# Two layer norms moved from VectorE to ScalarE, and the rotation of the keys from GpSimd to VectorE

## What is computed

```
x = x + layernorm(attention(layernorm(x)))
x = x + layernorm(ffn(layernorm(x)))

attention(x):                       # 16 heads of 128
    q = rope(x @ Wq.T)              # per head
    k, v = split(x @ Wkv.T)         # one key and one value for all heads
    kh, vh = running sums over the tokens of (x @ Wkvh.T) * exp(cumsum(log_sigmoid(x @ Wg.T)))
    k of head h = rope(k * kh[h]),  v of head h = v * vh[h]
    softmax(q k / sqrt(128), causal) v, heads joined, @ Wout.T
ffn(x):                             # 1024 hidden, ternary weights in groups of 64
    gate, up = split(x @ Wgu.T);  h = silu(gate) * up;  rms_norm(h) @ Wproj.T
layernorm(x) = (x - mean) / sqrt(var + 1e-5)
```

## Time and profile before

| | |
|---|---|
| time, median of 3 runs | 1162.76 us (1162.68 to 1162.89) |
| the profiled execution's own time | 1161.09 us |
| its span in the trace | 1159.3 us |
| PE busy | 1076.3 us (93% of the span), 7990 matmuls |
| PE weight loads busy | 1008.8 us (87%) |
| DVE busy | 874.5 us (75%) |
| ACT busy | 845.0 us (73%) |
| POOL busy | 914.9 us (79%) |
| clock granted to PE | full speed in nearly all slices |
| DMA | 50 GB/s on average |

### The profile page before, as it was taken

One profiled execution on the slowest core, in us unless ns is written; L12 is line 12 of the kernel. 1 busy time (PEld: TensorE's weight loads), 2 busy tenths in 40 slices (PEclk: granted clock), 3 DMA queues, 4 the chain that ended last, 5 costly groups with the idle time before them and its releaser, 6 DMA issues.

```text
span 1159.3 us, 26824 instructions
## 1 busy us (share of the span) xinstructions
PE 1076.3 (93%) x7990; PEld 1008.8 (87%) x7990; DVE 874.5 (75%) x2875; ACT 845.0 (73%) x2326; POOL 914.9 (79%) x845
## 2 busy tenths in 40 slices
PE   5799899989999999999899989999999899999996
PEld 4688898889888988898889888998988789999995
DVE  4578978897888779878987797878785656566563
ACT  2677777777777777787777777777777866666663
POOL 2687888797979797979798889888888647776774
PEclk8999999999999999999999999999999999999998
DMA  8260102010211111111011111111031000000000
GB/s 283 78 197 29 56 29 75 18 64 19 74 31 52 42 60 37 46 55 47 28 55 55 38 28 55 37 38 47 29 105 34 1 1 20 19 18 18 18 28 28
DMA packets 35192, 57.77 MB, mean 50 GB/s; under 512 B 3120, under 2 KB 15984, under 8 KB 34800
## 3 DMA queue, kind: packets, MB, share of 16 engines
q1 hardware_dynamic: 32912, 53.56, 14.9%
q10 hardware_dynamic: 2176, 3.15, 0.8%
HBM read 50.66 MB, written 9.18 MB: 52 GB/s over the span
## 4 chain that ended last, share of the span: by engine, by line
POOL 43%; issue 28%; PE 22%; ACT 3%; DVE 2%; DMA 1%; POOLq 1%; ACTq 0%; DVEq 0%; SPq 0%
POOL arena L526 13%; POOL arena L536 11%; POOL arena L547 9%; PE psum L835 8%; PE psum L852 6%; POOL arena L558 5%; PE psum L658 4%; POOL X L517 2%; ACT arena L1079 1%; PE psum L872 1%; POOL arena L503 1%; PE psum L753 1%; DVE pt_split L1318 1%; POOL arena L496 1%; PE psum L887 1%
## 5 line engine op out<-in xcount | busy, mean ns | idle before, releaser
L558 POOL TENSOR_TENSOR arena<-arena 128x768 f32<-128x768 f32 x128 | 188.2, 1470 | 106.7 <-DVE arena L1305 100.6
L526 POOL TENSOR_TENSOR arena<-arena,tables 128x512 f32<-128x512 f32 x128 | 174.4, 1363 | 17.5 <-ACT arena L979 17.5
L1318 DVE SCALAR_TENSOR_TENSOR pt_split<-psum,vh_col,pt_split 128x256 fp32r<-128x256 f32 (+1 forms) x512 | 187.3, 406 | 0.0
L753 PE MATMUL psum<-arena 128*128 128x256 f32 x512 | 157.6, 389 | 28.8 <-POOL arena L536 27.0
L536 POOL TENSOR_TENSOR arena<-arena 128x512 f32<-128x512 f32 x128 | 175.8, 1374 | 10.7 <-POOL arena L526 1.1
L990 ACT ACTIVATE arena<-arena 128x256 f32<-128x256 f32 x256 | 129.9, 507 | 74.4 <-DVE arena L1295 69.1
L547 POOL TENSOR_TENSOR arena<-arena 128x512 f32<-128x512 f32 x128 | 164.5, 1285 | 6.2 <-DMA arena<-kh_rows 6.2
L1280 DVE TENSOR_TENSOR arena<-psum,tables 128x512 f32<-128x512 f32 x128 | 86.1, 673 | 100.7 <-PE psum L658 95.2
L978 ACT ACTIVATE arena<-psum 64x512 f32<-64x512 f32 x128 | 76.1, 595 | 105.2 <-DVE arena L1280 105.1
L658 PE MATMUL psum<-wo_hi,o_hi 128*128 128x256 f32 x512 | 152.7, 298 | 0.0
L658 PE MATMUL psum<-xt_hi,wq_hi 128*128 128x256 f32 x512 | 146.9, 287 | 0.0
(11 more groups left out here) (161 smaller groups left out, 3511.5 us busy)
## 6 DMA issues: line engine op xcount, KB each, us to landing
arena<-kh_rows SPq DMA_DIRECT2D x128, 256.0 KB, 3.3
out<-spare SPq DMA_DIRECT2D x16, 256.0 KB, 2.1
arena<-w_rows SPq DMA_DIRECT2D x6, 512.0 KB, 4.3
X<-L_attn_Wout SPq DMA_DIRECT2D x1, 2048.0 KB, 14.8
X<-L_attn_x SPq DMA_DIRECT2D x1, 2048.0 KB, 9.5
w_rows<-L_ffn_w_gate_up ACTq DMA_DIRECT2D x4, 512.0 KB, 8.0
arena<-L_attn_Wq SPq DMA_DIRECT2D x1, 1536.0 KB, 10.4
X<-L_attn_x SPq DMA_DIRECT2D x1, 1536.0 KB, 15.7
```

The costliest lines, as they stand in the source:

```text
L526: nc.gpsimd.tensor_tensor(swap, swap, spread, ALU.mult).then_inc(q_sined, 1)
L558: nc.gpsimd.tensor_tensor(tb, tb, r.unsqueeze(3).to_broadcast([P, HP, 3, P]), ALU.mult).then_inc(p_ready, 1)
L753: nc.tensor.matmul(sj[:, 0:2 * P], q[:, j, P:N], kt[:, j, :], start=True, stop=True, skip_group_check=True)
L1318: last = nc.vector.scalar_tensor_tensor(pt_lo[p % 2][:, o], b[:, i], vh[:, t, h:h + 1], pt_hi[p % 2][:, o].bitcast(F32), ALU.mult, ALU.sub ...
```

## The change

Three things move.

1. `norm_x` (step 1) and `norm_y` (step 7) leave DVE. ACT applies them in two instructions each, as scale times input plus bias, with the inverse deviation as scale and minus mean times inverse deviation as bias, one value per partition. DVE computes that bias in one instruction of 128x2 each (`bias_x`, `bias_y`). On ACT, `norm_x` stands ahead of `swap` in step 1, `norm_y` behind `swap` in step 7.
2. `key_sin` and `key_rope` leave POOL for DVE, from steps 4 and 5 to steps 6 and 7, each behind the row maxima of its step.
3. Ahead of the first batch the same pieces move in the same way.

```diff
-FRONT = dict(stats=0, norm=1, turn=1, split=2, keys=3, gates=3, decay=4, coef=5, key_sin=4, key_rope=5, store=6,
+FRONT = dict(stats=0, norm=1, turn=1, split=2, keys=3, gates=3, decay=4, coef=5, key_sin=6, key_rope=7, store=6,
...
         @block.gpsimd
...
-            def key_sin(c0):
-                pool.wait_ge(k_swapped, c0 + PAIRS)
-                nc.gpsimd.tensor_tensor(k_swap, k_swap, sink, ALU.mult).then_inc(k_sin_done, PAIRS)
-            def key_rope(c0, par):
-                pool.wait_ge(k_sin_done, c0 + PAIRS)
-                pool.wait_ge(k_cos_done, c0 + PAIRS)
-                at_least(pool, k_scaled, c0 - PAIRS)
-                nc.gpsimd.tensor_tensor(keys[par], k_cos, k_swap, ALU.add).then_inc(k_ready, PAIRS)
...
         @block.scalar
...
+            def norm_x(c0):
+                xs = x_tiles(c0)
+                act.wait_ge(ln1_biased, c0 + PAIRS)
+                at_least(act, xt_turned, c0)
+                for t in range(NT):
+                    nc.scalar.activation(xn[:, t, :], xs[:, t, :], ACT.Identity, bias=ln1_bias[:, t:t + 1],
+                                         scale=ln1_rstd[:, t:t + 1]).then_inc(ln1_done, PAIRS // NT)
+            def norm_y(c0):
+                act.wait_ge(ln2_biased, c0 + PAIRS)
+                act.wait_ge(x1_done, c0 + PAIRS)
+                for t in range(NT):
+                    nc.scalar.activation(y_norm[:, t, :], y_sb[:, t, :], ACT.Identity, bias=ln2_bias[:, t:t + 1],
+                                         scale=ln2_rstd[:, t:t + 1]).then_inc(ln2_done, PAIRS // NT)
...
                     split_pt(g0, par, s)
+                    c0 = front_at(g0, s, "norm")
+                    if c0 is not None:
+                        norm_x(c0)
                     swap(g0, s)
+                    c0 = tail_at(g0, s, "norm")
+                    if c0 is not None:
+                        norm_y(c0)
...
             weight_hi(0)
+            norm_x(0)
             weight_hi(1)
...
         @block.vector
...
-            def norm_x(c0, par):
-                xs = x_tiles(c0)
+            def bias_x(c0):
                 dve.wait_ge(ln1_inv, c0 + PAIRS)
-                at_least(dve, xt_turned, c0)
-                for t in range(NT):
-                    nc.vector.scalar_tensor_tensor(xn[:, t, :], xs[:, t, :], ln1_agg[:, t, 0:1],
-                                                   ln1_rstd[:, t:t + 1].to_broadcast([P, E]), ALU.subtract, ALU.mult)\
-                        .then_inc(ln1_done, PAIRS // NT)
+                nc.vector.scalar_tensor_tensor(ln1_bias, ln1_agg[:, :, 0], -1.0, ln1_rstd, ALU.mult, ALU.mult)\
+                    .then_inc(ln1_biased, PAIRS)
...
+            def key_sin(c0):
+                dve.wait_ge(k_swapped, c0 + PAIRS)
+                nc.vector.tensor_tensor(k_swap, k_swap, sink, ALU.mult).then_inc(k_sin_done, PAIRS)
+            def key_rope(c0, par):
+                dve.wait_ge(k_sin_done, c0 + PAIRS)
+                dve.wait_ge(k_cos_done, c0 + PAIRS)
+                at_least(dve, k_scaled, c0 - PAIRS)
+                nc.vector.tensor_tensor(keys[par], k_cos, k_swap, ALU.add).then_inc(k_ready, PAIRS)
...
-            def norm_y(c0):
+            def bias_y(c0):
                 dve.wait_ge(ln2_inv, c0 + PAIRS)
-                dve.wait_ge(x1_done, c0 + PAIRS)
-                for t in range(NT):
-                    nc.vector.scalar_tensor_tensor(y_norm[:, t, :], y_sb[:, t, :], ln2_agg[:, t, 0:1],
-                                                   ln2_rstd[:, t:t + 1].to_broadcast([P, E]), ALU.subtract, ALU.mult)\
-                        .then_inc(ln2_done, PAIRS // NT)
+                nc.vector.scalar_tensor_tensor(ln2_bias, ln2_agg[:, :, 0], -1.0, ln2_rstd, ALU.mult, ALU.mult)\
+                    .then_inc(ln2_biased, PAIRS)
...
                     c0 = front_at(g0, s, "split_values")
                     if c0 is not None:
                         values_lo(c0, 1 - par)
+                    c0 = front_at(g0, s, "key_sin")
+                    if c0 is not None:
+                        key_sin(c0)
+                    c0 = front_at(g0, s, "key_rope")
+                    if c0 is not None:
+                        key_rope(c0, 1 - par)
...
             stats_x(0)
             gather_x(0)
+            bias_x(0)
             weight_lo(0)
             weight_lo(1)
-            norm_x(0, 0)
             split_x(0, 0)
...
             sum_kv(0, 0)
+            key_sin(0)
+            key_rope(0, 0)
             over_batches(dve, batch)
```

More of the change, by code:

```diff
@@ L206, in sandwich_kernel @@
         gate_mark = small[:, 84:86]
+        ln1_bias, ln2_bias = small[:, 86:88], small[:, 88:90]
         x2_stat = small3[:, 0:12].rearrange("p (t a) -> p t a", a=6)
@@ L236, in sandwich_kernel @@
         w_turned, w_hi_done, w_lo_done = sem("w_turned"), sem("w_hi_done"), sem("w_lo_done")
-        ln1_stats, ln1_aggr, ln1_eps, ln1_inv, ln1_done = (
-            sem(f"ln1_{k}") for k in ("stats", "aggr", "eps", "inv", "done"))
+        ln1_stats, ln1_aggr, ln1_eps, ln1_inv, ln1_biased, ln1_done = (
+            sem(f"ln1_{k}") for k in ("stats", "aggr", "eps", "inv", "biased", "done"))
         xt_turned, xt_hi_done, xt_lo_done = sem("xt_turned"), sem("xt_hi_done"), sem("xt_lo_done")
@@ L247, in sandwich_kernel @@
         kh_stored = sem("kh_stored")
-        y_copied, ln2_stats, ln2_aggr, ln2_eps, ln2_inv = (
-            sem(k) for k in ("y_copied", "ln2_stats", "ln2_aggr", "ln2_eps", "ln2_inv"))
+        y_copied, ln2_stats, ln2_aggr, ln2_eps, ln2_inv, ln2_biased = (
+            sem(k) for k in ("y_copied", "ln2_stats", "ln2_aggr", "ln2_eps", "ln2_inv", "ln2_biased"))
         ln2_done, x1_done = sem("ln2_done"), sem("x1_done")
@@ L632, in batch @@
                         invert_y(c0)
-                    c0 = front_at(g0, s, "key_sin")
-                    if c0 is not None:
-                        key_sin(c0)
-                    c0 = front_at(g0, s, "key_rope")
-                    if c0 is not None:
-                        key_rope(c0, 1 - par)
                     c0 = tail_at(g0, s, "add")
@@ L645, in _ @@
             pool.wait_ge(tables_in, 16)
-            key_sin(0)
-            key_rope(0, 0)
             over_batches(pool, batch)
@@ L1470, in batch @@
                     if c0 is not None:
-                        norm_x(c0, 1 - par)
+                        bias_x(c0)
                     c0 = vh_at(g0, s)
@@ L1488, in batch @@
                     if c0 is not None:
-                        norm_y(c0)
+                        bias_y(c0)
                     invert_sums(g0, s)
```

## The result

The changed kernel is slower by 0.2%: 1164.41 us median of 20 runs (1162.21 to 1165.73), beside 1162.2 us for the kernel before, measured again in the same rounds (20 runs, 1159.53 to 1163.14). The ratio is 1.002, with an interval from 1.0013 to 1.0027. The forecast was no change: -0.1 us, 1162.7 us on the first median of the kernel before.

A forecast was written before the change was run, and what follows sets the result against it. PE was taken to wait at step 0's scores for POOL's residual sum and the two instructions behind it. Terms -0.7 + 0 + 0 - 0.4 + 0.5 + 0.5 = -0.1 us gave 1162.7 us, range 1160.5 to 1165.5.

The forecast's parts named there:

- the path of `norm_y` in a plain batch: Step 7: from P (when PE could start scores) to scores 7.38 us against 7.47, 0.7 us gained over eight batches.
- POOL pays little, 1.35 us instead of 1.28: Beside a DVE instruction with two SBUF inputs, DVE waits its turn while POOL's instruction lengthens only from 1.28 to 1.35 us.
- norm_x on ACT, 0: Step 1: two ACT instructions, 1.08 us together, covered by ACT's wait for the cosines, so no change in time.
- Chunk batches, 0: Six chunk batches: cosines stay about 1.1 us late, path 8.5 instead of 8.20; 0 each, between -0.9 and +0.3.
- Behind the branch: After the loop's branch: key_rope overlaps DVE's 1.30 us idle time, costing 0, at most 1.5 us in five plain batches.
- Start, -0.4: Ahead of the first batch: norm_x on ACT no longer follows two DVE weight instructions; -0.4 us, between -0.6 and +0.5.
- End of attention, +0.5: After the last attention step: norm_y behind swap delays POOL's sum by 0.9 us, about half reaching the end; 0 to 0.9.
- Feed-forward, +0.5: Start of the feed-forward part: the last norm_y on ACT delays a pair PE needs; +0.5 us, between 0 and 1.1.
- PE hides 0.3 us: Step 0: PE hides about 0.3 us of the scores' lateness, as the output projection behind them waits anyway.
- DVE freed after all: Rival, chance 0.20: chunk batches' step 7 cosines come in time, 8.20 becomes 7.38, 4.9 us gained, 1157.8 us.
- key_rope and the branch add up: Rival, chance 0.22: the branch's 1.30 us start only after key_rope, costing 4 us over five batches, 1166.7 us.
- DVE's busy time down by 30 us: New profile: DVE's busy time was to fall by 30 us or more without effect on the kernel's time.

The follow-up runs named there:

- normy_ahead: The changed kernel with the call of norm_y on ACT moved ahead of swap in step 7, nothing else; median 1153.89 us, ratio 0.9926 to the kernel before.
- keys_pool: The changed kernel with all key instructions back on POOL, in the loop and ahead of it, norms still on ACT; median 1161.54 us, ratio 0.9999 to before.
- norms_dve: The changed kernel with both norms back on DVE, the keys staying on DVE; median 1162.29 us, ratio 1.0004 to the kernel before.
- sin_pool: The changed kernel with key_sin alone back on POOL at step 4 of the loop; median 1166.46 us, ratio 1.0044 to the kernel before.
- start_only: The kernel before with only the start changed: norm_x on ACT, key_sin and key_rope on DVE ahead of the first batch; median 1162.44 us, ratio 1.0016.
- ahead_res_step3: The changed kernel with norm_y ahead of swap and the chunk batches' residual sum moved to step 3 of the next batch; median 1148.18 us, ratio 0.9879 to before.

## Why the prediction was wrong

**The step that failed** is the size of the path of `norm_y` in a plain batch: "7.38 us from P ... against 7.47 a plain batch gains 0.09 us, and eight of them 0.7". The path itself was right: swap, `norm_y`, sum, sines, sum of the queries, scores. normy_ahead shows that it decides. Its length was not 7.38 but 7.73 us in the five batches of the loop and 7.50 to 7.54 in the last three, where the kernel before has 7.51 (7.47 to 7.54) and 7.35; I had put 7.47, the lowest of them, for all eight. Measured: +1.4 us for the eight batches instead of -0.7, which is 2.1 of the 2.3 us between the forecast and the measured difference. Of the 0.35 us that 7.73 is over 7.38:

- The handover from ACT to POOL takes 532.12 - 531.92 = 0.20 us, not 0.07. I had taken half of the way from POOL to PE for it.
- From the start of the sum to the scores it takes 536.42 - 532.12 = 4.30 us, not 4.12. That is L515 at 1.48 us instead of 1.29. `key_rope` was priced at 0 because DVE has time for it. It has, but it runs just beside POOL's instruction on the critical path, and POOL pays. In keys_pool, without `key_rope`, the product with the sines (L527 there) takes 1.28 us:

```profile
418.54 1.29 POOL L518 TENSOR_TENSOR X<-X,arena 128x512 f32 x1 [0.60 <-ACT arena L956]
419.79 1.28 POOL L527 TENSOR_TENSOR arena<-arena,tables 128x512 f32<-128x512 f32 x1
```

- The remaining 0.04 us are hundredths in swap and `norm_y`.

The prediction had "POOL pays little, 1.35 us instead of 1.28". Rows of the kernel before say otherwise: L536 takes 1.61 us in the earlier trace rows, and L526 takes 1.46 to 1.49 us in the 13 steps in which `norm_x` runs beside it, and 2.44 us beside two weight instructions:

```profile
460.30 2.44 POOL L526 TENSOR_TENSOR arena<-arena,tables 128x512 f32<-128x512 f32 x1
...
536.41 1.49 POOL L526 TENSOR_TENSOR arena<-arena,tables 128x512 f32<-128x512 f32 x1
```

The Trainium skill ("GPSIMD Engine Reference", section 8, Key points) has the contention that the first part of the prediction leaned on; I read it for DVE alone. The trace agrees for POOL too: 0.19 us more for each of the 14 products with the sines that start while `key_rope` still runs.

**The other terms.** *norm_x on ACT, 0*: right in the loop (norms_dve). *Chunk batches, 0*: right in sum (58.01 to 58.03), and by the parts given: the path through swap is 8.55 us where 8.5 was written, the cosines are 0.95 us late, and steps 5 to 7 are shorter in return (7.37 + 7.52 + 7.93 us to P of step 7, where 7.34 + 8.11 + 7.71 stood). *Behind the branch*: `key_rope` and the branch overlap. DVE waits 0.37 us here (0.37 to 0.58 in the five batches) where the earlier trace rows had 1.30, though in sin_pool they added up:

```profile
534.06 0.75 DVE L1186 BATCH_NORM_STATS2 arena<-X 128x6 f32 x2 [0.37 <-issue]
```

*Start, -0.4*: wrong in sign, +1.1 us by the medians of start_only (0.6 to 3.3, outside the -0.6 to +0.5 given); PE's first transposes did come earlier, at 7.57 us against 8.07 in the earlier trace rows, and it didn't help. *End of attention, +0.5*: measured +0.7, and 23.49 us, all of it back, with `norm_y` on DVE or ahead of `swap`. *Feed-forward, +0.5*: the last `norm_y` made PE start the product in question 40.40 us behind the part's first activation and not 39.83 (978.58 - 938.18, 972.98 - 933.15), 0.57 later as forecast, but the same product of the next sequence starts at 53.39 and 53.37, so nothing of it was left; the part as a whole got 0.8 shorter for another reason. *PE hides 0.3 us*: right. P of step 0 to P of step 1 is 6.72 us plus the lateness of the scores (6.72 + 0.93 = 7.65 before, 6.72 + 1.46 = 8.18 now), but never under 7.03, as normy_ahead (0.15 us late, 7.03) and ahead_res_step3 (0.0 late, 7.03) show. Behind a branch, with 0.24 to 0.27 us of lateness, it was 7.12 to 7.43 in normy_ahead.

The sum as measured: 0.8 + 0.6 + 0.7 - 0.8 + 1.1 = +2.4 us, with the two medians 2.2 us apart. That they meet so well is in part luck, since the start's term is known only as 0.6 to 3.3 us (the two profiles of each kernel have 2.0). The stretch behind the last sequence's first activation is not in it, since it differs between profiles of one kernel (15.20 and 16.33 us before).

**The rivals.** *DVE freed after all*: no, the cosines of step 7 were late. *key_rope and the branch add up*: against the kernel before the time came out nearer to it (+2.2, with +3.9 by the rival and -0.1 by the forecast), but not by its mechanism. The cosines of step 0 were 0.1 to 0.4 us late, under the 0.8 from which it would pay. It had the right instruction and the wrong victim. "DVE's busy time down by 30 us" was 874.5 to 859.4: the norms' 68.0 us left, but the two key instructions take 32.2 and the two bias instructions, 128x2 each, 23.4, since `bias_y` takes up to 1.25 us beside POOL.

```profile
L1280 DVE SCALAR_TENSOR_TENSOR arena<-arena x16: 148/698/1255, 137.0 to 975.3; 128x2 f32<-128x2 f32 x16
```

I also compared only the path that the change made with the one that it removed, and never asked whether ACT had an earlier slot. It had: `bias_y` was done at 528.22, 0.47 us ahead of P, and ahead of `swap` ACT stood idle for 0.31 us anyway, waiting for the cosines. `norm_y` there makes `swap` later, but what waits for `swap` has the time.

## What to carry to other kernels

When work moves to another engine, look at what waits for it, and put it ahead of whatever that engine does for a later customer: here one call placed behind `swap` and not ahead of it made a gain of 8 us a loss of 2. Price an instruction by what it does to the one that runs beside it on the other engine, not by its own engine's idle time alone; the trace of before can show that price. And read a difference in the start from several profiles of the same kernel, since here two of one kernel differed as much as two kernels did.

## What I had not expected of the hardware

- A handover from ACT to POOL took 0.20 us, three times my estimate, in the changed kernel's plain batch above, and 0.19 in keys_pool (418.54 - 417.25 - 1.10).
- The feed-forward part, whose instructions the change doesn't touch, takes 208.19, 208.25 and 208.27 us in the kernel before, its repeat and start_only, and 207.30 to 207.44 us in the thirteen others, whose loop is changed. Each pass of its loop gives 0.12 us, the first 0.37, at one instruction of DVE. In before:

```profile
1003.09 0.25 DVE L1412 BATCH_NORM_AGGREGATE arena<-arena 128x2 f32<-128x6 f32 x2
1003.77 0.69 DVE L1389 TENSOR_TENSOR arena<-arena,psum 128x512 f32<-128x512 f32 x1 [0.43 <-POOL wo_lo L564]
```

In the changed kernel:

```profile
1008.13 0.25 DVE L1422 BATCH_NORM_AGGREGATE arena<-arena 128x2 f32<-128x6 f32 x2
1008.44 0.69 DVE L1399 TENSOR_TENSOR arena<-arena,psum 128x512 f32<-128x512 f32 x1
```

The releaser named had long been done, and the cause stays open. It hid 0.8 us of the loss.
- Behind an idle stretch of PE of 5.1 and 5.6 us the granted clock was back at 1.00 from 30 us on in one profile of the kernel before, and still 0.50 from 34 to 35 us in the other.
